# Convolution plus gated projection on one core: the pair loop rotated, the set-up reordered

## The chip, the cores and the metric

The kernel runs on one core of one Trainium2 chip. The metric is the device time of one execution in microseconds (us); three executions of the kernel before took 694.74, 697.43 and 697.51 us, median 697.43.

## What is computed

Input x has 64 sequences, 64 heads and 1024 samples. Two layers follow one another, each added to its input:

```
y = x + (causal convolution of masked x with a 1024-tap kernel per head, built from
         64 complex modes: K = 2 Re sum_n C_n exp(dtA_n t), plus D * x), masked by length
base = y @ W.T                                    # 1024 x 1024
logits = y @ Wr.T + 5 * onehot(language)          # 8 experts
gates = softmax over the two largest logits
out = y + base + 2 * sum_e gates_e * (y @ A_e.T) @ B_e.T   # rank 16 per expert
```

## The kernel before

The heads are handled in 32 **pairs**; a pair is a tile of 128 tokens (two heads of 64 sequences) by 1024 samples in 8 chunks of 128. Every product is made in single precision out of three passes: operands are split into a high part (ACT, a copy rounded to fp32r) and a low part (DVE, the difference), and TensorE (PE) runs hi*hi, hi*lo, lo*hi. The names end in `_hi` and `_lo`.

For one pair PE does this: `turn_rows` (8 transposes of the input rows into `px`), `turn_powers` (2 transposes of the powers Z2 into `ct_psum`, from which come `c_hi`, `c_lo` and the first kernel samples `k_col`), `control` (6 matmuls: the states that enter each chunk, into `px`), `convolve` (6 matmuls with the Toeplitz block `t_hi`, `t_lo`, then 6 with the states `s_hi`, `s_lo`, into `pc`), and the projection: three banks of 24 matmuls with the stationary operand y and the moving operand [W, A, Wr] (1160 columns: bank 2 with the gates' columns first, then bank 0, then bank 1), and three matmuls per bank for the gated low-rank part (`add_lora`), which need the transposed gates.

Between PE's parts stand chains on the other engines. After `control`, ACT copies the states (`copy_states`) and DVE scans them (`scan_states`, eight steps in four pairs, the last three pairs each waiting for ACT to swap halves of the chunk just made, `swap_odd`); then ACT and DVE split them (`split_states`: s_hi, s_lo). After `convolve`, DVE merges the result into xt (`merge`), and ACT and DVE split that (`split_y`). After the first bank, DVE runs `route` (some fifteen small instructions; one waits for ACT's `ratio`), which ends in `gated`. After the banks, ACT copies them to `result` (`finish`, L487 to L488) and issues the output DMAs. Every second step (m = 0 and m = 1 of a loop turn) the powers of the next four heads are made as well: turns, magnitudes and `waves` on ACT at m = 0 (`waves` needs the sine table, L393), `powers`, `swap_powers`, `turn_powers` and `rotate_powers` at m = 1; at m = 1 a one-element Exp (`warm`, L569) brings the exponential table back.

The order of each engine is written by hand; all five engines run freely and wait on semaphores. The loop `Fori(0, LOOPS)` has LOOPS = 14 turns of two steps; step i is pair i's projection, and PE's order in it is: convolve(i+1), bank 2 of i, control(i+2), turn_powers(i+3), bank 0, bank 1 with the gates' transpose, turn_rows(i+3) and the low-rank parts inside it. DVE weaves other work between the four pairs of scan steps (L783): `split_ctr` and `split_obs` of the next pair but one, `split_toe` (t_lo, L749) and `split_gated`.

Ahead of the loop the set-up computes parameters on DVE (`par_step`), turns 11 weight tiles (`TILE`; W in 8 tiles, A, Wr, B) by `turn_weight`, each then split by ACT (`weight`, L370) and DVE (`low_weight`, L737), and convolves pair 0. Projection begins only in the loop, when all tiles are split.

## Time and profile before

| | |
|---|---|
| three executions | 694.74, 697.43, 697.51 us (median 697.43) |
| profiled execution | 695.72 us, of which the span from first to last instruction is 693.9 us |
| PE matmul busy | 645.8 us (93%), 3621 instructions |
| DVE busy | 490.0 us (71%) |
| ACT busy | 467.8 us (67%) |
| mean granted TensorE clock | 0.974 of full |

Time outside the span is 1.8 us. In the rows further down the first number is the start in us from the span's start, the second the duration; "[a <-b]" is the idle time of the engine just before and what ended it. Instructions that follow one another without a wait overlap by about 0.1 us, so that distances between starts, not durations, add up.

### The profile page before, as it was taken

To read this page: it belongs to the slowest core of one execution; us is meant where nothing else is said; L and a number is where in the kernel's file an instruction comes from. 1 tells how busy PE (TensorE), PEld (TensorE's weight loads), DVE (VectorE), ACT (ScalarE), POOL (GpSimd) and SP (SyncE) were. 2 spreads that over 40 slices of the span, in tenths; PEclk is the share of its full clock that TensorE was granted. 3 is DMA by queue.
4 is the path that set the end of the run, shared out by engine and by line. 5 is a ranking of instruction groups with operands and counts; after the bars stand their busy time and mean duration, and the time that the engine had idled before them with its cause. 6 is when DMAs were issued, how large, how long until landed. Compare 5 with 4: busy or idle time off the path is not lost.

```text
span 693.9 us, 12598 instructions
## 1 busy us (share of the span) xinstructions
PE 645.8 (93%) x3621; PEld 615.2 (89%) x3621; DVE 490.0 (71%) x1531; ACT 467.8 (67%) x973; POOL 20.4 (3%) x46
## 2 busy tenths in 40 slices
PE   3364999999999999999999999999999999999997
PEld 2353899999999999999999999999999999999997
DVE  8876567777776767777776767777776767777621
ACT  4784577677768677677768677777768677675411
POOL 2000000000000000000000000000000000000000
PEclk9875899999999999999999999999999999999999
DMA  7123023222123233223123233223123223221112
GB/s 241 49 69 89 11 68 70 54 52 68 32 67 68 68 68 68 53 53 68 31 68 68 68 68 68 53 53 68 31 68 68 68 68 68 53 53 39 31 32 60
DMA packets 22869, 43.36 MB, mean 62 GB/s; under 512 B 8104, under 2 KB 13512, under 8 KB 22856
## 3 DMA queue, kind: packets, MB, share of 16 engines
q1 hardware_dynamic: 17576, 26.42, 17.1%
q10 hardware_dynamic: 5280, 16.78, 9.5%
q14 instruction: 7, 0.06, 0.1%
q8 instruction: 6, 0.10, 0.1%
HBM read 26.35 MB, written 16.84 MB: 62 GB/s over the span
## 4 chain that ended last, share of the span: by engine, by line
DVE 36%; ACT 25%; issue 18%; PE 13%; ACTq 6%; DMA 2%; DVEq 1%; SPq 0%
DVE state L783 17%; PE pmg L1104 9%; ACTq L470 5%; ACT result L488 4%; ACT u_hi L416 4%; ACT turn L379 3%; ACT L393 3%; DVE y_lo L830 3%; ACT swapped L439 2%; ACT Z L405 2%; DVE Z L770 2%; ACT xt L413 2%; DVE c_lo L764 2%; ACT z_swap L398 2%; PE pc L1029 2%
## 5 line engine op out<-in xcount | busy, mean ns | idle before, releaser
L1104 PE MATMUL pmg<-w_hi,y_hi 128*128 128x388 f32 (+1 forms) x768 | 268.7, 350 | 1.7 <-ACT result L488 0.2
L1104 PE MATMUL pmg<-w_hi,y_lo 128*128 128x388 f32 (+1 forms) x768 | 260.1, 339 | 0.0
L1104 PE MATMUL pmg<-w_lo,y_hi 128*128 128x388 f32 (+1 forms) x768 | 259.8, 338 | 0.0
L1104 PEld LDWEIGHTS pmg<-w_hi,y_hi 128*128 128x128 f32 x768 | 144.3, 188 | 7.5 <-ACT result L488 6.5
L1104 PEld LDWEIGHTS pmg<-w_hi,y_lo 128*128 128x128 f32 x768 | 144.6, 188 | 0.2
L1104 PEld LDWEIGHTS pmg<-w_lo,y_hi 128*128 128x128 f32 x768 | 144.2, 188 | 0.0
L439 ACT ACTIVATE swapped<-state 64x128 f32<-64x128 f32 x192 | 59.3, 309 | 67.1 <-DVE state L783 65.7
L783 DVE SCALAR_TENSOR_TENSOR state<-swapped,scan_tab,state 128x192 f32<-128x192 f32 (+1 forms) x240 | 73.8, 349 | 12.1 <-ACT swapped L439 0.2
L812 DVE TENSOR_TENSOR s_lo<-state,s_hi 128x896 fp32r<-128x896 f32 x32 | 35.0, 1093 | 31.5 <-ACT s_hi L461 31.5
L744 DVE TENSOR_TENSOR u_lo<-xt,u_hi 128x1024 fp32r<-128x1024 f32 x32 | 39.2, 1225 | 24.8 <-ACT u_hi L416 24.8
L461 ACT ACTIVATE s_hi<-state 128x896 fp32r<-128x896 f32 x32 | 30.5, 953 | 35.0 <-DVE state L783 35.0
L783 DVE SCALAR_TENSOR_TENSOR state<-state,scan_tab 128x64 f32<-128x64 f32 x180 | 50.6, 323 | 0.0
L770 DVE SCALAR_TENSOR_TENSOR Z<-z_swap,gen_tab,Z 128x128 f32<-128x128 f32 x56 | 16.0, 347 | 38.8 <-ACT Z L405 38.8
L824 DVE COPY_PREDICATED xt<-valid,pc 128x512 f32<-128x512 int32 x64 | 42.9, 724 | 0.0
L488 ACT ACTIVATE result<-pmg 128x388 f32<-128x388 f32 (+1 forms) x96 | 37.0, 458 | 8.1 <-PE pmg L1079 7.9
L466 ACT ACTIVATE y_hi<-xt 128x1024 fp32r<-128x1024 f32 x32 | 33.5, 1048 | 13.2 <-DVE xt L824 13.2
L830 DVE TENSOR_TENSOR y_lo<-xt,y_hi 128x1024 fp32r<-128x1024 f32 x32 | 39.0, 1220 | 4.0 <-ACT y_hi L466 3.9
L379 ACT ACTIVATE turn<-pos,phase,gen_tab 128x128 f32<-128x128 f32 x56 | 23.1, 484 | 22.6 <-issue 22.6
L1022 PE MATMUL px<-ident,rows 128*128 128x128 f32 x256 | 35.8, 286 | 0.0
L398 ACT ACTIVATE z_swap<-Z 64x512 f32<-64x512 f32 x32 | 20.2, 630 | 19.5 <-issue 19.0
L1022 PEld LDWEIGHTS px<-ident,rows 128*128 128x128 f32 x256 | 32.1, 149 | 1.2
L413 ACT ACTIVATE xt<-px 128x1024 f32<-128x1024 f32 x31 | 31.3, 1010 | 0.7 <-PE px L1022 0.7
(195 smaller groups left out, 1068.1 us busy)
## 6 DMA issues: line engine op xcount, KB each, us to landing
rows<-in_x SPq DMA_DIRECT2D x64, 256.0 KB, 5.1
out<-result ACTq DMA_DIRECT2D x62, 256.0 KB, 3.0
toe<-kpad SPq DMA_DIRECT2D x32, 128.0 KB, 4.5
result<-in_L_cond_W SPq DMA_DIRECT2D x5, 512.0 KB, 7.2
rows<-in_L_cond_W SPq DMA_DIRECT2D x2, 512.0 KB, 7.8
result<-in_L_cond_A SPq DMA_DIRECT2D x1, 512.0 KB, 5.8
b_rows<-in_L_cond_B SPq DMA_DIRECT2D x1, 512.0 KB, 7.0
xt<-in_L_cond_W SPq DMA_DIRECT2D x1, 512.0 KB, 8.8
```

The source lines that it names most:

```text
L379: ins = nc.scalar.activation(turn[:, h, :], pos[:, :], ACT.Identity, bias=phase[:, 0:1], scale=gen_scalar(TURNS, g, h, staged))
L413: nc.scalar.activation(xt[s][:, :, :], px[:, :, :], ACT.Copy).then_inc(xt_ready, 1)
L439: ins = nc.scalar.activation(swapped[out_half, :, chunks, :], source[in_half, :, chunks, :], ACT.Copy)
L470: act.dma_start(bass.AP(out.tensor, (2 * i + h) * LEN + c0, [[HEADS * LEN, SEQS], [1, c1 - c0]]), result[s][h * SEQS:(h + 1) * SEQS, c0:c1 ...
L488: nc.scalar.activation(result[s][:, c0:c1], pm[:, n, 0:c1 - c0], ACT.Copy).then_inc(pm_free, 1)
L744: vec.tensor_tensor(u_lo[s][:, :, :], xt[s][:, :, :], u_hi[s][:, :, :].bitcast(F32), ALU.subtract).then_inc(ulo_ready, 1)
L783: ins = vec.scalar_tensor_tensor(out=state[:, h, chunks, :], in0=source[:, h, at, :], scalar=scan_scalar(name, m if staged else i, h, staged),
L812: vec.tensor_tensor(s_lo[:, :, :, :], state[:, :, :, :], s_hi[:, :, :, :].bitcast(F32), ALU.subtract).then_inc(slo_ready, 1)
L824: ins = vec.copy_predicated(xt[s][:, :, h * SEQS:(h + 1) * SEQS], valid[:, :, :], pc[:, h, :, :])
L830: vec.tensor_tensor(y_lo[s][:, :, :], xt[s][:, :, :], y_hi[s][:, :, :].bitcast(F32), ALU.subtract).then_inc(ylo_ready, 1)
L1022: ins = nc.tensor.transpose(px[:, c, :], rows[s][:, c * P:(c + 1) * P], ident[:, :])
L1104: ins = nc.tensor.matmul(pm[:, n, 0:c1 - c0], y[s][:, c, :], w[:, c, c0:c1], start=(c == 0 and y is y_hi and w is w_hi), stop=(c == CH - 1 ...
```

## The change

**The loop is rotated.** PE's step i is now: turn_powers(i+2), bank 2 of i, bank 0 of i, the gates' transpose (`turn_gates`), convolve(i+1), the low-rank parts of those two banks, control(i+2), bank 1 with turn_rows(i+3) in it. On DVE the scan of pair i+2 runs in one piece behind split_y(i+1), and the next step begins with split_ctr and split_obs, then (m = 1) powers, route, split_rows, split_toe, split_gated and merge. On ACT `finish` is taken apart: the third bank of a pair is copied in the next step (`evacuate`), its DMAs are issued in `store`, `waves` stands ahead of the first two banks' copies, and `warm` has moved from m = 1 to m = 0, between the last `swap_odd` and split_states.

**Two steps are peeled** ahead of the loop (which now has 13 turns from b = 1), each in an order of its own.

**The set-up** is rewritten. A second exact exponential on DVE (14 instructions, `decay_exp`) becomes one ACT Exp. The low part of pair 0's rows is taken from `px` itself; the first two heads' powers go ahead of the other two; the first samples of the first two pairs' kernels come as rows (`kernel_row`: two matmuls with the selector `pick`, through the DRAM tensor `kpad_rows`); B is sorted by ACT and no longer by POOL. W has one more staging buffer (`w0_rows`), and the tiles have another order: those of bank 2 first (A, W6, W7, Wr), and pair 0's banks are projected between the later tiles' transposes, chunk ranges of `project`. DVE's order there is: low parts of tiles 4 to 9 around the scan of pair 1, powers(1) behind tile 9, then route(0, 0), tile 10, merge(0, 1); on ACT the copies of pair 0's first two banks stand ahead of split_y(0, 1) and split_rows(0, 2).

The core of the diff (PE's, DVE's and ACT's steps, PE's set-up):

```diff
-        TILE = [(A_, in_pm, 0), (B_, in_pc, 0), (W_, in_pm, 6), (W_, in_pc, 0), (WR_, in_pm2, 0), (W_, in_pm, 7),
-                (W_, in_pc, 1), (W_, in_pm, 2), (W_, in_pc, 3), (W_, in_pm, 4), (W_, in_pc, 5)]
+        TILE = [(A_, in_pm, 0), (W_, in_pc, 6), (W_, in_pm, 7), (WR_, in_pm2, 0), (W_, in_pm, 0), (W_, in_pc, 1),
+                (W_, in_pm, 2), (W_, in_pc, 3), (W_, in_px, 4), (B_, in_pc, 0), (W_, in_px, 5)]
...
+            store_row(0)
+            sp.wait_ge(pad_stored, 64)
+            load_toe_rows(0)
...
+            sp.wait_ge(px_full, 2)
+            load_w(5)
+            sp.wait_ge(wt_full, w_tile(0) + 1)
+            load_w(4)
             sp.wait_ge(wt_full, w_tile(1) + 1)
             load_rows(0, 2)
-            sp.wait_ge(wt_full, w_tile(2) + 1)
-            load_w(4)
+            sp.wait_ge(wt_full, w_tile(5) + 1)
+            load_rows(0, 3)
...
-            def step(b, m, rows_left=True, ahead=True, kernels=True):
+            copy_states(0, 2)
+            for n in range(3):
+                swap_odd(0, 2, n)
+            split_states(0, 2)
+
+            split_ctr(0, 3)
+            split_obs(0, 3)
+            evacuate(0, 0, 2)
+            split_rows(0, 3)
+            ratios(0, 1)
+            split_toe(0, 2)
+            act.wait_ge(gen_staged, 1)
+            turns_of(None, True)
+            magnitudes(None, True)
+            store(0, 0)
+            split_gated(0, 1)
+            waves(2)
+            evacuate(0, 1, 0)
+            evacuate(0, 1, 1)
+            split_y(0, 2)
+            copy_states(0, 3)
+            swap_odd(0, 3, 0)
+            swap_powers(2)
+            swap_odd(0, 3, 1)
+            turn_powers(2, True)
+            swap_odd(0, 3, 2)
+            nc.scalar.activation(warm[:, :], phase[:, 0:1], ACT.Exp)
+            split_states(0, 3)
+
+            def step(b, m, rows_left=True, kernels=True):
+                if rows_left:
+                    split_ctr(b, m + 2)
+                    split_obs(b, m + 2)
+                evacuate(b, m - 1, 2)
+                if rows_left:
+                    split_rows(b, m + 2)
+                ratios(b, m)
+                split_toe(b, m + 1)
                 if kernels and m == 0:
                     act.wait_ge(gen_staged, b + 1)
                     turns_of(None, True)
                 if kernels and m == 1:
                     swap_powers(b + 2)
-                    turn_powers(b + 2, True)
-                split_y(b, m + 1)
+                store(b, m - 1)
+                split_gated(b, m)
                 if kernels and m == 0:
                     magnitudes(None, True)
+                    waves(b + 2)
                 if kernels and m == 1:
-                    nc.scalar.activation(warm[:, :], phase[:, 0:1], ACT.Exp)
-                ratios(b, m)
+                    turn_powers(b + 2, True)
+                for j in range(2):
+                    evacuate(b, m, j)
+                split_y(b, m + 1)
                 if rows_left:
                     copy_states(b, m + 2)
-                if ahead:
-                    split_ctr(b, m + 3)
-                    split_obs(b, m + 3)
-                if rows_left:
-                    swap_odd(b, m + 2, 0)
-                    split_toe(b, m + 2)
-                    swap_odd(b, m + 2, 1)
-                split_gated(b, m)
-                if rows_left:
-                    swap_odd(b, m + 2, 2)
+                    for n in range(3):
+                        swap_odd(b, m + 2, n)
+                    if kernels and m == 0:
+                        nc.scalar.activation(warm[:, :], phase[:, 0:1], ACT.Exp)
                     split_states(b, m + 2)
-                if ahead:
-                    split_rows(b, m + 3)
-                if kernels and m == 0:
-                    waves(b + 2)
-                finish(b, m)
-
-            with act.Fori(0, LOOPS) as b:
+
+            with act.Fori(1, LOOPS) as b:
                 for m in range(2):
                     step(b, m)
             step(LOOPS, 0, kernels=False)
...
+            next(scanning)
+            split_toe(0, 0, toe_rows_back)
...
+            vec.tensor_copy(len_f[:, :], len_i[:, :]).then_inc(masks, 1)
+            vec.tensor_copy(lang_f[:, :], lang_i[:, :]).then_inc(masks, 1)
+            split_states(0, 0)
             dve.wait_ge(masks, 2)
             vec.tensor_tensor(valid[:, :, :], sample_no[:, :].unsqueeze(2).to_broadcast([P, CH, SEQS]),
                               len_f[:, :].unsqueeze(1).to_broadcast([P, CH, SEQS]), ALU.is_lt).then_inc(masks, 1)
...
-            def step(b, m, rows_left=True, ahead=True, kernels=True):
+            dve.wait_ge(scan_staged, 1)
+            for _ in scan_states(0, 2):
+                pass
+            split_states(0, 2)
+
+            split_ctr(0, 3)
+            split_obs(0, 3)
+            route(0, 1)
+            split_rows(0, 3)
+            split_toe(0, 2)
+            angles(2)
+            split_gated(0, 1)
+            merge(0, 2)
+            powers(2)
+            split_y(0, 2)
+            for _ in scan_states(0, 3):
+                pass
+            rotate_powers(2, True)
+            split_states(0, 3)
+
+            def step(b, m, rows_left=True, kernels=True):
+                if rows_left:
+                    split_ctr(b, m + 2)
+                    split_obs(b, m + 2)
                 if kernels and m == 1:
                     powers(b + 2)
-                merge(b, m + 1)
+                route(b, m)
+                if rows_left:
+                    split_rows(b, m + 2)
+                split_toe(b, m + 1)
                 if kernels and m == 0:
                     angles(b + 2)
+                split_gated(b, m)
+                merge(b, m + 1)
                 if kernels and m == 1:
                     rotate_powers(b + 2, True)
                 split_y(b, m + 1)
-                route(b, m)
-                scanning = iter(())
                 if rows_left:
                     dve.wait_ge(scan_staged, b + m // 2 + 1)
-                    scanning = scan_states(b, m + 2)
-                next(scanning, None)
-                if ahead:
-                    split_ctr(b, m + 3)
-                    split_obs(b, m + 3)
-                next(scanning, None)
...
-                next(scanning, None)
-                if rows_left:
+                    for _ in scan_states(b, m + 2):
+                        pass
                     split_states(b, m + 2)
-                if ahead:
-                    split_rows(b, m + 3)
-
-            with dve.Fori(0, LOOPS) as b:
+
+            with dve.Fori(1, LOOPS) as b:
                 for m in range(2):
...
+            def turn_gates(b, m, tables_split):
+
+                pe.wait_ge(gated_ready, 2 * b + m + 1)
+                pe.wait_ge(clo_ready, tables_split)
+                nc.tensor.transpose(pg[:, 0:P], gated[:, :, :].rearrange("p e r -> p (e r)"), ident[:, :]
+                                    ).then_inc(gt_full, 1)
+
+            def add_loras(b, m):
+
+                pe.wait_ge(gthi_ready, 2 * b + m + 1)
+                pe.wait_ge(gtlo_ready, 2 * b + m + 1)
+                add_lora(BANK_ORDER[0])
+                add_lora(BANK_ORDER[1])
+
...
@@ -1117,50 +1249,101 @@
             pe.wait_ge(par_dve, C2_STEPS)
             pe.wait_ge(prm_ready, 1)
             turn_parameters(C2_RE)
+            pe.wait_ge(z2_half, 1)
             pe.wait_ge(prm_ready, 2)
-            turn_powers(0, 0)
+            turn_powers(0, 0, first=True)
+            pe.wait_ge(tables, 2)
+            kernel_row(0)
+            pe.wait_ge(xt_ready, 1)
             control(0, 0)
-            pe.wait_ge(k_ready, 1)
+            pe.wait_ge(clo_ready, 1)
             turn_powers(0, 1)
+            kernel_row(1)
             turn_weight(2)
+            turn_rows(0, 1)
+            pe.wait_ge(k_ready, 2)
             turn_weight(3)
-            turn_rows(0, 1)
+            pe.wait_ge(wlo_ready, 2)
+            convolve(0, 0, first=True)
             turn_weight(4)
-            turn_weight(5)
-            convolve(0, 0, first=True)
             control(0, 1)
             pe.wait_ge(merged, 1)
+            turn_weight(5)
+
+            wait_y(0, 0)
+            pe.wait_ge(wlo_ready, 4)
+            project(0, 0, 0, 0, 3)
             turn_weight(6)
-            pe.wait_ge(k_ready, 2)
-            pe.wait_ge(clo_ready, 2)
+            project(0, 0, 0, 3, 6)
+            turn_weight(7)
+            pe.wait_ge(v_copied, 2)
+            pe.wait_ge(scan, SCAN + 1)
+            turn_weight(8)
+            project(0, 0, 0, 6, 8)
+            pe.wait_ge(wlo_ready, w_tile(3) + 1)
+            project(0, 0, 1, 0, 4)
+            turn_weight(9)
+            project(0, 0, 1, 4, 8)
+            turn_weight(10)
+            pe.wait_ge(wlo_ready, 10)
+            convolve(0, 1)
+            turn_gates(0, 0, 2)
+            pe.wait_ge(wlo_ready, WTILES)
+            project(0, 0, 2, 0, 4)
+            turn_rows(0, 2)
+            project(0, 0, 2, 4, 7)
+            add_loras(0, 0)
+            project(0, 0, 2, 7, 8)
+            add_lora(BANK_ORDER[2])
             turn_powers(0, 2)
-            for k in range(7, WTILES):
-                turn_weight(k)
-            turn_rows(0, 2)
-
...
+            wait_y(0, 1)
+            project(0, 1, 0, 0, 4)
+            turn_rows(0, 3)
+            project(0, 1, 0, 4, 8)
+            project(0, 1, 1)
+            turn_gates(0, 1, 4)
+            convolve(0, 2)
+            add_loras(0, 1)
+            control(0, 3)
+            project(0, 1, 2, 0, 7)
+            turn_rows(0, 4)
+            project(0, 1, 2, 7, 8)
+            add_lora(BANK_ORDER[2])
+
+            def step(b, m, rows_left=True, ahead=True):
+                if rows_left:
+                    turn_powers(b, m + 2)
+                wait_y(b, m)
+                project(b, m, 0)
+                project(b, m, 1)
+                turn_gates(b, m, 2 * b + m + 3 if rows_left else PAIRS)
                 convolve(b, m + 1)
-                pe.wait_ge(yhi_ready, 2 * b + m + 1)
-                pe.wait_ge(ylo_ready, 2 * b + m + 1)
-                project_bank(b, m, 0)
+                add_loras(b, m)
                 if rows_left:
                     control(b, m + 2)
+                project(b, m, 2, 0, 7)
                 if ahead:
-                    turn_powers(b, m + 3)
-                project_bank(b, m, 1)
-                project_bank(b, m, 2, ahead)
-
-            with pe.Fori(0, LOOPS) as b:
+                    turn_rows(b, m + 3)
+                project(b, m, 2, 7, 8)
+                add_lora(BANK_ORDER[2])
+
+            with pe.Fori(1, LOOPS) as b:
                 for m in range(2):
                     step(b, m)
-            step(LOOPS, 0, kernels=False)
-            step(LOOPS, 1, ahead=False, kernels=False)
-            step(LOOPS + 1, 0, rows_left=False, ahead=False, kernels=False)
-            pe.wait_ge(yhi_ready, PAIRS)
-            pe.wait_ge(ylo_ready, PAIRS)
-            for j in range(3):
-                project_bank(LOOPS + 1, 1, j)
```

**Place 1, DVE in the loop, step m = 0 before** (L783 scan, L749 t_lo, L868 gt_lo; "waits" names semaphores):

```order
L783 SCALAR_TENSOR_TENSOR state<-swapped,scan_tab,state 128x64 [waits swap_ready]
L783 SCALAR_TENSOR_TENSOR state<-swapped,scan_tab,state 128x64
L749 TENSOR_TENSOR t_lo<-toe,t_hi 128x256 [waits thi_ready]
L796 REGISTER_ALU
L783 SCALAR_TENSOR_TENSOR state<-state,scan_tab 128x64 [waits scan]
L783 SCALAR_TENSOR_TENSOR state<-state,scan_tab 128x64
```

t_lo stands here inside the scan. The same engine and turn of the change, step m = 1 (where the former row order had the scan's pieces between these), from split_states on:

```order
L914 TENSOR_TENSOR s_lo<-state,s_hi 128x896 [waits shi_ready]
L855 REGISTER_ALU
L857 TENSOR_REDUCE k_col<-pmg 128x2 [waits chi_ready]
L858 TENSOR_TENSOR c_lo<-pmg,c_hi 128x256
L848 SCALAR_TENSOR_TENSOR zo_lo<-Z,sigma,zo_hi 128x256 [waits zhi_ready]
L723 ISA [waits mag_ready,sin_ready]
L725 TENSOR_TENSOR Z<-angle,mag 128x512 [waits z_swapped,zlo_ready]
L940 TENSOR_TENSOR logits<-pmg,bias 128x8 [waits gate_done]
```

k_col, c_lo and zo_lo have moved from the scan to behind s_lo, and route behind them. The same step of the change from route's last instruction on:

```order
L964 TENSOR_TENSOR gated<-pmg,gates 128x128 [waits router]
L837 TENSOR_TENSOR u_lo<-xt,u_hi 128x1024 [waits uhi_ready,xt_ready]
L842 TENSOR_TENSOR t_lo<-toe,t_hi 128x256 [waits thi_ready]
L970 TENSOR_TENSOR gt_lo<-pmg,gt_hi 128x128 [waits gthi_ready]
L918 COPY held<-lang_f 128x1 [waits conv_done,ulo_ready]
L926 COPY_PREDICATED xt<-valid,pc 128x8x64 x2
```

The Toeplitz block's low part has moved from the middle of the scan to a place behind the whole scan, split_states, route and split_rows.

**Place 2, PE in the loop**, the convolution and what stands ahead of it, before and of the change (L1079 is the low-rank part, L1230 the gates' transpose):

```order
L1079 MATMUL pmg<-bt_hi,gt_hi 128x388
L1079 MATMUL pmg<-bt_hi,gt_lo 128x388
L1079 MATMUL pmg<-bt_lo,gt_hi 128x388
L1029 MATMUL pc<-u_hi,t_hi 128x512 [waits tlo_ready,merged,thi_ready,wlo_ready,ulo_ready,uhi_ready]
L1029 MATMUL pc<-u_lo,t_hi 128x512
```

Here the previous pair's last low-rank matmuls are followed by the convolution. PE of the change:

```order
L1229 REGISTER_ALU [waits gated_ready]
L1230 MATMUL pmg<-ident,gated 128x128 [waits clo_ready]
L1165 REGISTER_ALU
L1159 MATMUL pc<-u_hi,t_hi 128x512 [waits tlo_ready,thi_ready,merged,ulo_ready,uhi_ready]
L1159 MATMUL pc<-u_lo,t_hi 128x512
```

The convolution has moved from the step's head to behind the gates' transpose; it still waits for t_lo.

**Place 3, ACT in the loop**, the table load before (step m = 1, ahead of ratio), and of the change (step m = 0, ahead of s_hi):

```order
L466 ACTIVATE y_hi<-xt 128x1024 [waits merged]
L569 ACT_TABLE_LOAD
L569 ACTIVATE warm<-phase 128x1
L474 ISA
L475 ACTIVATE ratio<-top 128x1 [waits router]
```

Here it stands behind y_hi. ACT of the change:

```order
L479 ACTIVATE swapped<-state 64x2x64
L668 ACT_TABLE_LOAD
L668 ACTIVATE warm<-phase 128x1
L498 REGISTER_ALU
L501 ACTIVATE s_hi<-state 128x896 [waits conv_done,scan]
```

The load has moved from beside split_y to between the last swap and the split of the states.

## Rows read from the trace of the kernel before

**Rows 1.** The page's 40 slices of the span, PE's busy tenths and granted clock

```profile
PE   3364999999999999999999999999999999999997
...
PEclk9875899999999999999999999999999999999999
```

**Rows 2.** The timeline of DVE in the set-up: start, duration, engine, line

```profile
47.63 1.22 DVE L830 TENSOR_TENSOR y_lo<-xt,y_hi 128x1024 fp32r<-128x1024 f32 x1 [0.56 <-ACT y_hi L466]
...
73.34 1.22 DVE L737 TENSOR_TENSOR w_lo<-pc,w_hi 128x1024 fp32r<-128x1024 f32 x1 [4.10 <-ACT w_hi L370]
```

**Rows 3.** The timeline of PE in the loop and near the end

```profile
113.33 0.39 PE L1029 MATMUL pc<-u_hi,t_hi 128*128 128x512 f32 x1
...
308.58 0.39 PE L1029 MATMUL pc<-u_hi,t_hi 128*128 128x512 f32 x1
...
311.18 0.34 PE L1104 MATMUL pmg<-w_hi,y_hi 128*128 128x384 f32 x1
...
315.39 0.36 PE L1029 MATMUL px<-u_hi,c_hi 128*128 128x448 f32 x1
...
327.72 0.39 PE L1029 MATMUL pc<-u_hi,t_hi 128*128 128x512 f32 x1
...
347.63 0.39 PE L1029 MATMUL pc<-u_hi,t_hi 128*128 128x512 f32 x1
...
658.03 0.39 PE L1029 MATMUL pc<-u_hi,t_hi 128*128 128x512 f32 x1
```

**Rows 4.** The timeline of DVE near the end, where it waits for others

```profile
649.90 0.74 DVE L783 SCALAR_TENSOR_TENSOR state<-state,scan_tab,px 128x192 f32<-128x192 f32 x2 [0.57 <-ACT swapped L439]
...
652.19 0.48 DVE L783 SCALAR_TENSOR_TENSOR state<-swapped,scan_tab,state 128x64 f32<-128x64 f32 x2 [0.25 <-ACT swapped L439]
...
660.89 0.15 DVE L816 COPY held<-lang_f 128x1 f32<-128x1 f32 x1 [3.10 <-PE pc L1029]
660.96 1.34 DVE L824 COPY_PREDICATED xt<-valid,pc 128x512 f32<-128x512 int32 x2
```

**Rows 5.** The timeline of DVE in the loop

```profile
302.20 0.28 DVE L763 TENSOR_REDUCE k_col<-pmg 128x2 f32<-128x128 f32 x1
...
303.12 0.47 DVE L783 SCALAR_TENSOR_TENSOR state<-state,scan_tab 128x64 f32<-128x64 f32 x2
...
308.29 1.09 DVE L812 TENSOR_TENSOR s_lo<-state,s_hi 128x896 fp32r<-128x896 f32 x1 [1.02 <-ACT s_hi L461]
...
316.74 0.16 DVE L838 TENSOR_TENSOR logits<-pmg,bias 128x8 f32<-128x8 f32 x1
...
319.01 0.74 DVE L783 SCALAR_TENSOR_TENSOR state<-state,scan_tab,px 128x192 f32<-128x192 f32 x2
...
...
330.49 0.69 DVE L635 TENSOR_TENSOR Z<-angle,mag 128x512 f32<-128x512 f32 x1 [0.81 <-ACT angle L393]
```

**Rows 6.** The timeline of ACT in the loop

```profile
307.30 0.95 ACT L461 ACTIVATE s_hi<-state 128x896 fp32r<-128x896 f32 x1 [1.10 <-DVE state L783]
...
309.07 1.01 ACT L416 ACTIVATE u_hi<-px 128x1024 fp32r<-128x1024 f32 x1
...
314.41 1.04 ACT L466 ACTIVATE y_hi<-xt 128x1024 fp32r<-128x1024 f32 x1
...
317.40 0.58 ACT L447 ACTIVATE state<-px 128x512 f32<-128x512 f32 x1
317.99 0.98 ACT L439 ACTIVATE swapped<-px 64x384 f32<-64x384 f32 x2
...
336.21 1.28 ACT L569 ACT_TABLE_LOAD   x1
337.50 0.20 ACT L569 ACTIVATE warm<-phase 128x1 f32<-128x1 f32 x1
```

**Rows 7.** The waits, whole span: total us, times, longest us

```profile
ACT turn L379 <- issue: 22.6, 13, 1.8
...
ACT z_swap L398 <- issue: 19.0, 14, 1.5
```

488 lines of the change are left out of this document (273 added, 215 removed).

## The prediction

> **What bounds the kernel now.** I read the page's slices first. From the sixth of 40 slices on PE is busy to nine tenths or more at the full granted clock; in the first five it is busy to three to six tenths, and there its clock falls to between 5 and 8 tenths [rows 1]. So there are two places: a set-up of some 75 us that PE waits through, and a loop that PE's own work fills. In the set-up pair 0 is ready for projection at 48.85 us (its y_lo starts at 47.63 and takes 1.22), but the last weight tile's low part ends only at 74.56 [rows 2]: 26 us in which the projection could run and does not.
>
> In the loop I take the start of each convolution as the mark. One step lasts 19.14 us (308.58 to 327.72) and the next 19.91 (to 347.63), 39.05 for a turn of two [rows 3]. The first is PE's work alone. The second holds 0.77 of waiting, around the powers and a late copy on ACT. PE's own pace would be 38.28 a turn.
>
> **What the change does to the order.** The convolution now stands behind two banks, one of which takes 4.21 (311.18 to 315.39) [rows 3]. At the same mark 8.4 us less work is left than before. PE does the same matmuls otherwise; the two selector products and the halves of B cost under 1 us, in a set-up where PE waits anyway. The end (last bank, copy, store) is as before.
>
> **The loop.** The question is whether DVE and ACT close their circle within PE's 19.14. The circle begins at a convolution and ends at the next, because that one waits for t_lo, and DVE makes t_lo only behind the whole scan, split_states, route and split_rows. Counted from the convolution's first matmul:
> - The merge's first instruction comes at 2.86 (658.03 to 660.89) and the merge ends at 4.27 [rows 3, 4]. y_hi follows at 4.31; ACT's next instruction can start 0.95 later (1.04 less an overlap of 0.09), the copy of the states is 0.59 and the swaps 0.98 [rows 6], so the scan starts at 6.86. control's result is there by 4.9 (the low-rank parts and six matmuls behind the convolution), so ACT, not PE, sets this.
> - The scan, now in one piece: 2.29 to the first addition that waits for a swap (649.90 to 652.19) [rows 4]. That addition is 0.48; the next pair takes 0.03 + 0.73 + 0.48 in the same way (0.73 is 2.29 less two steps of 0.78), and the last pair, with no swap left to wait for beyond its first half, 0.03 + 0.78 + 0.75. Sum 5.57. s_hi starts at 12.46.
> - From s_hi: s_lo 0.99 later, the next instruction 1.00 after that [rows 5, 6], k_col, c_lo and zo_lo together 0.92 (302.20 to 303.12). Then route: 2.27 from logits to the instruction behind it (316.74 to 319.01) [rows 5]. u_lo, as large as y_lo [rows 2], 1.13 net; t_lo, a quarter of it, about 0.4; 0.1 until PE starts.
> - At m = 1 powers comes ahead of route, 0.60 (0.69 less 0.09) [rows 5]. 12.46 + 0.99 + 1.00 + 0.92 + 0.60 + 2.27 + 1.13 + 0.4 + 0.1 = 19.87.
> - At m = 0 route waits for ratio. On ACT s_hi and xt take 1.77 (307.30 to 309.07), u_hi 0.91 [rows 6], and between them stand three copies of 256, 256 and 388 columns, about 1.1 (an estimate from xt's 0.91 for 1024): ratio can start 3.8 behind s_hi, and route wants it at 3.5. The loop's turn adds 0.38 on ACT: the idle time that nothing explains is 22.6/13 = 1.74 at the turn and 19.0/14 = 1.36 within it [rows 7]. So 0.68 in place of powers' 0.60: 19.95.
> - warm now stands between the last swap and s_hi, once a turn. From that swap's start s_hi would come after 1.64; with the load of 1.28 and the 0.20 [rows 6] it comes after 2.2. That is 0.5.
>
> Sum 40.3 a turn against 39.05, **1.27 more**. Of this PE is idle 2.0, ahead of each convolution. The former 0.77 goes and is worth nothing. Bounds: at best the three estimated pieces and the register instructions hide each other (0.8 less); at worst the scan's additions in the loop carry another 0.1 each and the waves at m = 0 delay y_hi (0.8 more). The 13 turns between the third mark and the 29th: **+16.5** (6 to 27). The two steps behind it have no powers: +0.4.
>
> A rule against this: the Trainium skill (ScalarE: Activation LUTs, What ACT_TABLE_LOAD costs) has a drain of about 1.38 us beside the load's 1.28. Here the load starts at 336.21, and warm at 337.50, 0.01 behind its end; no row shows the drain [rows 6]. With it warm's 0.5 would be some 1.9.
>
> **The set-up.** Here I followed DVE, ACT and PE through the new orders, each instruction with its duration from before.
> - The 14 dropped DVE instructions (about 0.13 apart) and the split powers bring pair 0's first convolution forward. Pair 0's y_lo is done at about 41, 8 us earlier than in [rows 2].
> - Between 36 and 63 DVE has seven low parts of 1.13, the scan and the splits of pair 1, merge, angles, powers(1) and route, some 23 us of work, and powers(1) must wait for ACT's exponentials. The last tile is split at about 63, 11 us earlier than in [rows 2]. Two of pair 0's banks run beside this, hidden.
> - Then bank 1 of pair 0 (4.3), the turned rows and the low-rank parts end at 69. ACT copies two banks before it makes y_hi of pair 1 and then xt and u_hi of pair 2; DVE's u_lo and c_lo follow, and control of pair 2 starts at 74.3 with PE idle since 70. The slices show the clock at 5 tenths after such holes [rows 1], so it takes 2.3 instead of 1.2. Copy, scan and the chain above (1.6 + 5.6 + 7.1) bring pair 2's convolution, the second mark, to 91.0.
> - The next step carries swap_powers, turn_powers and rotate_powers inside the scan, 1.85 more than 19.95: the third mark falls at 112.8, before 113.33 [rows 3]: **-0.5**. The set-up's 8 to 11 us are spent again in these two steps. Bounds -5 and +4: pieces of the set-up hide better, or half clock again in the next convolution.
>
> **Sum.** 693.9 - 8.4 - 0.5 + 16.5 + 0.4 = 701.9 of span, with the 1.8 outside it 703.7, against the profiled execution's 695.72. Its time lies inside the three runs shown, 1.7 under their median, so I leave the sum at its level: **704 us**, 1% over the median. A measurement here can tell about 0.5% from no change: faster is under 694, slower over 701.
>
> **Rivals.**
> - *The loop stays PE's* (0.23). If some part of the circle overlaps that I put in a row, the third and later marks keep 39.05: 704 - 16.5 = 687.5, and at PE's own 38.28 677.5. The circle must be 1.0 shorter a step than I count, out of 20. For it: DVE is busy for 71% only. Against it: the waits in the chain are of the kind that rows 4 to 6 show, each with its idle time. It gives faster for 0.20 and same for 0.03.
> - *The clock falls in the loop* (0.06). Each step now has a hole of about 1 us at full clock; the trace of before has none there, and shows falls only in the set-up [rows 1]. A convolution of 2.60 (308.58 to 311.18) [rows 3] takes as much again at half clock (1.2 GHz), in 26 steps 68: 772.
> - *A dearer table switch* (0.04). If ACT empties for about another load's length, 1.28, before the load that now has idle neighbours, 13 x 1.28 = 16.6 is added: 720. The rule of the Trainium skill's ScalarE: Activation LUTs (What ACT_TABLE_LOAD costs) would bring it.
> - *The set-up does not do what it says* (0.05). If the rewritten order stalls (staging buffers are freed late, or the strided copy of B), pair 0's banks wait for tiles as they did and only the loop's loss remains: 704 + 8 = 712 or more.
> - *My forecast* (0.62), with its own range of 694 to 716: 0.50 over 701, 0.12 under.
>
> **Numbers.** Faster 0.20; same 0.12 + 0.03 = 0.15; slower 0.50 + 0.06 + 0.04 + 0.05 = 0.65. The range leaves out the clock's case, the top of the dear cases and the lower half of the first rival: 686 to 717.
>
> **What would show it.** PE's timeline of the change: idle times of 0.7 to 1.5 ahead of each convolution's first matmul, released by DVE's t_lo; two marks 40.3 apart over a turn (under 39.0 I am wrong about the circle); s_hi a further 0.5 behind the last addition at m = 0 with the table load ahead of it; DVE with idle times only where it waits for ACT inside the scan. In the set-up: y_lo of pair 0 ending near 41, the last low part near 63, a hole in PE near 70 to 74, pair 3's convolution near 113. PE idle nowhere ahead of the convolution, or the granted clock under full in the loop, would each prove a rival.

## The result and the profile after

The changed kernel takes 714.6 us (median of 4 executions, 714.37 to 714.98), the kernel before 696.36 in the same session (4 executions): a ratio of 1.0264, 95% interval 1.0238 to 1.0291. It is slower, as forecast, but by 2.6% and not by 1%. Its profiled execution took 714.37 us, the span is 712.6 against 693.9.

| | forecast | measured | miss |
|---|---|---|---|
| third mark against before (112.8 forecast, 120.23 measured, 113.33 before) | -0.5 | +6.9 | +7.4 |
| 13 loop turns between the third and the 29th mark | +16.5 | +19.4 | +2.9 |
| from there to the end | -8.0 | -7.6 | +0.4 |
| span | 701.9 | 712.6 | +10.7 |

The marks are again the first matmuls of the convolutions; the 29th is at 647.18, and was at 620.87 in the kernel before. The timeline of PE of the changed kernel (start, duration; idle time before and its releaser in brackets), rows that answer to [rows 3]:

```profile
91.80 0.76 PE L1159 MATMUL pc<-u_hi,t_hi 128*128 128x512 f32 x1 [1.34 <-DVE t_lo L842]
...
120.23 0.47 PE L1159 MATMUL pc<-u_hi,t_hi 128*128 128x512 f32 x1
...
303.07 0.47 PE L1159 MATMUL pc<-u_hi,t_hi 128*128 128x512 f32 x1 [1.27 <-DVE t_lo L842]
...
322.91 0.47 PE L1159 MATMUL pc<-u_hi,t_hi 128*128 128x512 f32 x1 [0.47 <-DVE t_lo L842]
...
343.61 0.47 PE L1159 MATMUL pc<-u_hi,t_hi 128*128 128x512 f32 x1 [1.27 <-DVE t_lo L842]
...
647.18 0.47 PE L1159 MATMUL pc<-u_hi,t_hi 128*128 128x512 f32 x1 [0.48 <-DVE t_lo L842]
```

Steps of 19.84 and 20.70 alternate; the turn is 40.54 long ((647.18 - 120.23) / 13 = 40.53), where it was (620.87 - 113.33) / 13 = 39.04. In the loop every convolution waits for t_lo, released by DVE. The page's list of waits says the same for the whole span, and shows the one long wait for powers that the forecast had not:

```profile
PE pc L1159 <- DVE t_lo L842: 28.9, 29, 4.3
PE pmg L1201 <- DVE Z L864: 4.2, 1, 4.2
PE px L1159 <- DVE c_lo L858: 4.0, 1, 4.0
```

The slices, against [rows 1]: PE is fuller early (the banks of pair 0 run there), but the fifth and sixth slices fall to 7, and the granted clock is low in two separate stretches of the set-up. In the loop it is full, holes and all.

```profile
PE   3679778999999999999999999999999999999997
...
PEclk9699988999999999999999999999999999999999
```

**The circle in the loop.** The timeline of DVE between the marks 322.91 and 343.61, the step that ends at m = 1:

```profile
325.86 0.15 DVE L918 COPY held<-lang_f 128x1 f32<-128x1 f32 x1 [1.93 <-PE pc L1159]
...
329.96 0.74 DVE L885 SCALAR_TENSOR_TENSOR state<-state,scan_tab,px 128x192 f32<-128x192 f32 x2 [0.33 <-ACT swapped L479]
...
336.90 1.09 DVE L914 TENSOR_TENSOR s_lo<-state,s_hi 128x896 fp32r<-128x896 f32 x1 [1.40 <-ACT s_hi L501]
337.91 0.28 DVE L857 TENSOR_REDUCE k_col<-pmg 128x2 f32<-128x128 f32 x1
...
338.95 0.69 DVE L725 TENSOR_TENSOR Z<-angle,mag 128x512 f32<-128x512 f32 x1
339.56 0.16 DVE L940 TENSOR_TENSOR logits<-pmg,bias 128x8 f32<-128x8 f32 x1
...
341.80 1.22 DVE L837 TENSOR_TENSOR u_lo<-xt,u_hi 128x1024 fp32r<-128x1024 f32 x1
342.93 0.42 DVE L842 TENSOR_TENSOR t_lo<-toe,t_hi 128x256 fp32r<-128x256 f32 x1
```

And ACT's part of the same step:

```profile
327.31 1.06 ACT L506 ACTIVATE y_hi<-xt 128x1024 fp32r<-128x1024 f32 x1
...
333.87 0.63 ACT L479 ACTIVATE swapped<-state 64x128 f32<-64x128 f32 x2 [0.55 <-DVE state L885]
334.52 1.28 ACT L668 ACT_TABLE_LOAD   x1
335.82 0.20 ACT L668 ACTIVATE warm<-phase 128x1 f32<-128x1 f32 x1
335.93 0.94 ACT L501 ACTIVATE s_hi<-state 128x896 fp32r<-128x896 f32 x1
```

Link by link, measured (forecast): convolution to merge 2.95 (2.86), to y_hi 1.45 (1.45), to the scan 2.65 (2.55), scan to s_hi 5.97 (5.60 and 0.5 for the warming Exp), to s_lo 0.97 (0.99), to k_col 1.01 (1.00), to powers 1.04 (0.92), powers 0.61 (0.60), route 2.24 (2.27), u_lo 1.13 (1.13), t_lo and PE's start 0.68 (0.5). Sum 20.70 against 20.37.

**The set-up.** Pair 0's y_lo starts at 39.47 and the last low part at 63.30, 1.2 long each, so that they end at 40.7 and 64.5 (forecast 41 and 63); the second mark is 91.80 (91.0). From there to the third mark it takes 28.43 where 21.8 was forecast. PE's timeline there, then the stretches' busy time (PE first) and granted clock (the 0.50 and 0.78 behind POOL's entry), for the convolution and for the banks in front of the third mark:

```profile
75.61 0.44 PE L1159 MATMUL px<-u_hi,c_hi 128*128 128x448 f32 x1 [4.03 <-DVE c_lo L858]
...
109.09 0.69 PE L1201 MATMUL pmg<-ident,Z 128*128 128x128 f32 x2 [4.20 <-DVE Z L864]
```

```profile
91.80:96.73 4.93, 4.93 (x12) 4.09 (x13) 0.97 (x3) 1.88 (x2) 0.00 (x0) 0.50 0.56 135
109.78:120.20 10.42, 10.42 (x50) 10.38 (x48) 5.58 (x21) 5.16 (x11) 0.00 (x0) 0.78 0.41 84
```

At half the clock, its 1.2 GHz level, the 12 matmuls take 4.93 and not 2.60. And the turn of the powers, with which PE's peeled step (1, 0) begins, stands 4.20 idle with two banks queued behind it, because DVE's rotate_powers(2) comes behind the whole scan of pair 3:

```profile
105.80 0.75 DVE L885 SCALAR_TENSOR_TENSOR state<-state,scan_tab 128x192 f32<-128x192 f32 x2
107.24 0.75 DVE L885 SCALAR_TENSOR_TENSOR state<-swapped,scan_tab,state 128x192 f32<-128x192 f32 x2 [0.69 <-ACT swapped L479]
107.90 1.14 DVE L864 SCALAR_TENSOR_TENSOR Z<-z_swap,gen_tab,Z 128x128 f32<-128x128 f32 x4
```

### The profile page after: what moved, and what is told of

Its sections match the earlier page's. It is cut to its first block, busy times and chain, and to the rows that moved or that the text cites. A ratio compares the mean times of both kernels' runs of the same rounds, so it can differ in the third digit from the quotient of the medians.

```text
span 712.6 us, 12371 instructions
## 1 busy us (share of the span) xinstructions
PE 648.1 (91%) x3629; PEld 617.4 (87%) x3629; DVE 495.3 (70%) x1518; ACT 464.9 (65%) x980; POOL 19.1 (3%) x38
## 4 chain that ended last, share of the span: by engine, by line
DVE 34%; PE 22%; issue 21%; ACT 21%; DVEq 1%; ACTq 1%; DMA 0%; SPq 0%
PE pc L1159 13%; DVE state L885 11%; ACT swapped L479 9%; PE pmg L1220 7%; DVE xt L926 5%; ACT s_hi L501 3%; DVE u_lo L837 3%; ACT state L487 3%; ACT L668 2%; DVE t_lo L842 2%; DVE zo_lo L848 2%; DVE gate L959 1%; DVE held L918 1%; DVE k_col L857 1%; DVE c_lo L858 1%
## 5 line engine op out<-in xcount | busy, mean ns | idle before, releaser
L1220 PEld LDWEIGHTS pmg<-w_hi,y_hi 128*128 128x128 f32 x768 | 145.9, 190 | 4.1 <-DVE w_lo L828 3.6
L524 ACT ACTIVATE result<-pmg 128x388 f32<-128x388 f32 (+1 forms) x96 | 43.2, 452 | 71.8 <-PE pmg L1207 71.3
L918 DVE COPY held<-lang_f 128x1 f32<-128x1 f32 x96 | 14.8, 154 | 78.5 <-PE pc L1159 76.3
L1159 PE MATMUL pc<-u_hi,t_hi 128*128 128x512 f32 x64 | 28.7, 448 | 28.9 <-DVE t_lo L842 28.9
L1159 PEld LDWEIGHTS pc<-u_hi,t_hi 128*128 128x128 f32 x64 | 12.4, 194 | 36.7 <-issue 35.2
L1152 PE MATMUL px<-ident,rows 128*128 128x128 f32 x256 | 34.1, 277 | 1.1 <-DVE state L885 1.1
L1152 PEld LDWEIGHTS px<-ident,rows 128*128 128x128 f32 x256 | 30.5, 144 | 2.4 <-issue 1.2
L456 ACT ACTIVATE u_hi<-px 128x1024 fp32r<-128x1024 f32 x31 | 32.0, 1033 | 0.0
```

Source lines behind the costliest of these rows:

```text
L524: nc.scalar.activation(result[s][:, c0:c1], pm[:, n, 0:c1 - c0], ACT.Copy).then_inc(pm_free, 1)
L1152: ins = nc.tensor.transpose(px[:, c, :], rows[s][:, c * P:(c + 1) * P], ident[:, :])
L1159: ins = nc.tensor.matmul(out, l, r, start=first and n == 0, stop=last and n == 2, skip_group_check=True)
L1220: ins = nc.tensor.matmul(pm[:, n, 0:o1 - o0], y[s][:, c, :], w[:, c, o0:o1], start=(c == 0 and y is y_hi and w is w_hi), stop=(c == CH - 1 ...
```

## The experiments

All are edits of the changed kernel; ratios are to the kernel before in the same session. Times of different sessions are compared below where the text says "less" or "slower", and the kernel before had medians of 696.27 to 697.58 in them: a difference of 1 us between two such times says nothing by itself.

**1. toe_first: t_lo ahead of u_lo.** The circle's theory says that the loop's loss hangs on what stands ahead of t_lo. DVE's step:

```diff
                 route(b, m)
+                split_toe(b, m + 1)
                 if rows_left:
                     split_rows(b, m + 2)
-                split_toe(b, m + 1)
```

> One swap on DVE: in every loop step t_lo is made ahead of u_lo of the next pair but one, so 1.13 us earlier. Theory (the next convolution waits for t_lo at the end of DVE's and ACT's circle): the step into m = 0 loses its wait of 0.48 and the step into m = 1 loses 1.13 of its 1.27; a turn falls from 40.53 to about 38.95 us, the span by 13 x 1.58 + 0.5 + 0.5 = 21.5, the time to about 693. Rival (PE's new order itself, or its matmuls being longer, costs the turn): the turn stays near 40.5 and the time near 714.

Measured 690.95 us, ratio 0.9901 (0.9876 to 0.9926): one line moved turns 2.6% of loss into 1% of gain. A turn lasts 38.70, a little less than the 38.95 expected.

**2. toe_early: t_hi and t_lo right behind the splits of zo, ahead of powers, route and the rows' split.** On ACT t_hi goes behind zo_hi, on DVE

```diff
+                split_toe(b, m + 1)
                 if kernels and m == 1:
                     powers(b + 2)
                 route(b, m)
                 if rows_left:
                     split_rows(b, m + 2)
-                split_toe(b, m + 1)
```

> t_hi (ACT) and t_lo (DVE) are made right behind the next pair but one's zo, ahead of powers, route and the rows' split, some 4 us earlier than in the change. Theory: the wait ahead of each convolution is gone in both steps and the turn is PE's own, about 38.8 us (19.43 + 19.36 from the change's trace); time about 691. If another link of the circle (the gates' transpose, the states' low part) is late next, the turn stays above 39 and PE's wait moves to that instruction. Rival (PE's order costs): 714.

Measured 690.06, ratio 0.9904 (0.9886 to 0.9922), no better than the first. PE's timeline shows no idle time ahead of the convolutions.

```profile
312.89 0.48 PE L1159 MATMUL pc<-u_hi,t_hi 128*128 128x512 f32 x1
...
332.46 0.47 PE L1159 MATMUL pc<-u_hi,t_hi 128*128 128x512 f32 x1
```

Steps of 19.57 and 19.13 alternate, a turn of 38.70 against 40.54: 13 x 1.84 = 23.9 of the 24.5 us. The two former waits, 1.27 and 0.47, are gone in both experiments. The step of 19.57 is still 0.45 longer than the other, and not by PE's own work: here the gates' transpose ahead of its convolution starts 0.40 behind the last matmul of the bank (331.82 to 332.22; in the other step 0.19), and the convolution 0.24 behind the transpose (0.02). In toe_first the transpose is on time (334.31), and the convolution starts 0.46 behind it. In either order DVE's route and t_lo both stand ahead of this convolution, which fits the equal turns. Experiment 10 takes this step up again.

**3. late_turn: the turn of the powers behind the first bank, in the peeled step only.**

```diff
-                if rows_left:
+                if rows_left and not late:
                     turn_powers(b, m + 2)
                 wait_y(b, m)
                 project(b, m, 0)
+                if late:
+                    turn_powers(b, m + 2)
                 project(b, m, 1)
...
-            with pe.Fori(1, LOOPS) as b:
+            step(1, 0, late=True)
+            step(1, 1)
+            with pe.Fori(2, LOOPS) as b:
```

> Only PE's order in the loop's first step changes: the transposes of pair 4's powers stand behind that step's first bank instead of at its head. Theory for the third mark (pair 3's convolution at 120.23 us in the change's trace, 7.4 later than predicted): PE waited 4.2 us at its head for rotate_powers(2), which DVE makes behind the whole scan, with two banks queued behind the wait; now the first bank runs in that wait, the convolution comes at about 115.5, bound by DVE's chain again, and the time falls by 4.8 to about 709.7. Rival (the late third mark is the half clock and the slow convolution at 91.8 alone): third mark at 119 to 120, time 714.

Measured 709.81, ratio 1.0192 (1.0171 to 1.0212): 4.8 less. The wait for the powers is gone (107.49, no idle time), the third mark comes 23.18 behind the second, not 28.43, and the convolution waits for t_lo as in the loop:

```profile
107.49 0.44 PE L1201 MATMUL pmg<-ident,Z 128*128 128x128 f32 x2
...
114.36 0.47 PE L1159 MATMUL pc<-u_hi,t_hi 128*128 128x512 f32 x1 [1.34 <-DVE t_lo L842]
```

With the late turn the circle of DVE and ACT binds this step again. Its 23.18 is 1.4 more than the 21.8 forecast, and the convolution at its head took 3.86 (91.18 to 95.04, granted clock 0.66) where 2.60 is its length at full clock: that is 1.3 of it.

**4. no_warm: the warming Exp left out.** The line with `warm` in ACT's loop is deleted; the load then falls to ratio at m = 1.

> The one-element Exp between the last swap and the states' high part at m = 0 is left out; the table load then stands ahead of ratio at m = 1 (the result is the same). Theory: s_hi at m = 0 comes 0.5 us earlier, but ratio at m = 1 about 1.0 later than route wants it, so the step into m = 1 is about 0.5 longer than 20.70 and the time about 720. If a table switch costs a further drain of the order of 1.4 us beside its 1.28, the step is longer by that again (some 738). If s_hi was not bound by warm, the step grows by 1.0 (727).

Measured 723.77 in a single run, 9.2 slower. The step that ends at m = 1 lasts 21.28 instead of 20.70, 7.5 in 13 turns; the third mark comes 0.9 earlier (119.29). Another 2.9 come from two of the other steps, which last 21.40 (from 140.57) and 21.13 (from 347.69) and not 19.84: the granted clock was 0.92 over each, and 0.55 from 140.57 to 143.00. Both times PE had just waited 0.43 and 1.27; the other turns of this kernel have the same two waits, and their steps keep 21.28 and 19.84. The load now stands on the path to route:

```profile
301.77 1.28 ACT L510 ACT_TABLE_LOAD   x1
303.06 0.30 ACT L510 ACTIVATE ratio<-top 128x1 f32<-128x1 f32 x1
```

Where it stood, load and Exp cost 0.40 (the scan's start to s_hi is 5.97 with them and 5.57 in the other step of the same trace, 350.64 to 356.21). Here the step is 0.58 longer although these 0.40 are saved, so 0.98 show. The next instruction starts 0.01 behind the load's end, here as in the changed kernel: the dear switch is out.

**5. early_late: 2 and 3 together.**

> Two edits at once: t_hi and t_lo early in the steps of the loop (alone 690.06), and PE's turn of the powers behind the first bank in its peeled first step (alone 4.8 under the changed kernel, 709.81 against 714.6). The first takes 1.84 from each turn of the loop, the second only from the stretch between the convolutions of pair 2 and pair 3, so they should add: 690.06 - 4.8 = 685.3, with loop turns of 38.70. If instead the 4.8 was only won because the loop's DVE behind it was late anyway (the loop of that kernel waits for t_lo), or if PE's order there only moves the wait, 690.0.

Measured 685.89, ratio 0.9844 (0.9827 to 0.9861). The two losses, loop and peeled step, add: 4.2 of the second's 4.8 are left on top of the first.

**6. act_order: in ACT's set-up, pair 1's y_hi ahead of the copies of pair 0's banks.**

```diff
-            evacuate(0, 0, 0)
-            evacuate(0, 0, 1)
             split_y(0, 1)
             split_rows(0, 2)
+            evacuate(0, 0, 0)
+            evacuate(0, 0, 1)
```

> The changed kernel with one thing altered in ACT's set-up: y_hi of pair 1 and the copy and u_hi of pair 2 stand ahead of the two bank copies of pair 0 instead of behind them. ACT waits 3.18 idle for the first bank's last LoRA there, while the merged rows of pair 1 have been ready since about 65.2; y_hi could start near 65.9 and not 69.8, c_lo of pair 2 end near 71 and not 74.6, and PE's hole of 4.03 ahead of control(0,2) close to under 1. Theory (ACT's order makes the hole): control(0,2) starts at about 71.5, the second mark moves from 91.8 to about 88, and the whole kernel gains 3.5 to 5 (the stretch at half clock behind the hole may go too): 710.5. Rival (the next limit, the copies of the banks moved behind, holds project(0,1,0) back as long, or the time is lost at the next wait for gates): 713.5 or more.

Measured 711.67, ratio 1.0211 (1.0191 to 1.0231): 2.9 less, between theory and rival. The hole of 4.03 is down to 1.22 and the second mark comes at 89.17 (from 91.80), but a part came back at the next wait: the gates of pair 1, for which PE now waits 2.88 and not 1.92.

**7. fill: PE's two waits ahead of the convolution of pair 2 filled.** It adds work that computes nothing:

```diff
             project(0, 1, 1)
+            pe.wait_ge(clo_ready, 4)
+            for n in range(34):
+                nc.tensor.transpose(ct_psum[:, n % 2, :], ident[:, :], ident[:, :])
             turn_gates(0, 1, 4)
             convolve(0, 2)
```

> The changed kernel with 34 transposes of the identity added to PE's two waits ahead of the convolution of pair 2 (idle 1.92 and 1.34 there; 34 x 0.10 = 3.4). They compute nothing. Theory: that convolution took 4.93 and not 2.6 because the granted clock was 0.50 behind the two waits; with the waits filled it starts at 91.9 and takes about 2.7, the merge of pair 2 comes 2.2 earlier, and the kernel ends 2 earlier: 712.4. Rival 1: the clock falls all the same (it was 0.66 and 0.72 in two other kernels with the same waits), and nothing changes: 714.6. Rival 2: the filler only delays the gates' turn and what follows by its overshoot: 715.5.

Measured 711.72, ratio 1.0215 (1.0198 to 1.0232): PE does more and the kernel ends 2.9 earlier. The convolution's stretch at full clock (1.00), 2.66 long where it was 4.93, and the banks ahead of the third mark at 0.86:

```profile
91.34:94.00 2.66, 2.65 (x12) 2.32 (x13) 0.98 (x3) 2.05 (x3) 0.00 (x0) 1.00 0.67 90
107.00:116.50 9.50, 9.50 (x49) 9.50 (x48) 5.57 (x21) 5.17 (x11) 0.00 (x0) 0.86 0.32 61
```

The wait for the powers stays, 4.43. So the 6.6 us have two causes that are now each shown alone, this and experiment 3. How far the clock falls is not steady, but that it falls is: in eight kernels with both waits left (1.92 to 2.88 and 1.20 to 1.37) the 12 matmuls of this convolution took 4.93 or 4.94 at 0.50 (the changed kernel, toe_first, early_late, act_order, warm_gap) or 3.86 to 3.88 at 0.66 (toe_early, late_turn, no_warm); in none of them did the convolution as a whole run at full clock.

**8. full: 2, 3 and 6, and t of pair 2 ahead of its route in the set-up.**

> All orders together: t early in the loop (-24.5), PE's late turn of the powers in its peeled step (-4.8), ACT's y_hi and u_hi ahead of the bank copies in the set-up (-4), and t_hi and t_lo of pair 2 ahead of the route in the set-up (-1.3, the wait ahead of the convolution of pair 2): 714.6 - 34.6 = 680.0. If the set-up's orders overlap (what ACT's order wins is lost at the gates of pair 1, whose route stands behind the scan of pair 2): 684.

Measured 680.39, ratio 0.9763 (0.9748 to 0.9778), as the sum said. Between the control of pair 2 and the third mark one long wait of PE's is left, for the gates of pair 1:

```profile
87.90 0.47 PE L1230 MATMUL pmg<-ident,gated 128*128 128x128 f32 x1 [3.21 <-DVE gated L964]
88.11 0.77 PE L1159 MATMUL pc<-u_hi,t_hi 128*128 128x512 f32 x1
...
104.49 0.44 PE L1201 MATMUL pmg<-ident,Z 128*128 128x128 f32 x2 [0.24 <-DVE Z L864]
```

**9. warm_gap: the warming Exp behind the copy of the states,** where ACT idles for 1.67 (alone, in the changed kernel):

```diff
                     copy_states(b, m + 2)
+                    if kernels and m == 0:
+                        nc.scalar.activation(warm[:, :], phase[:, 0:1], ACT.Exp)
                     for n in range(3):
                         swap_odd(b, m + 2, n)
-                    if kernels and m == 0:
-                        nc.scalar.activation(warm[:, :], phase[:, 0:1], ACT.Exp)
```

> The changed kernel with the warming Exp of the loop put behind the copy of the states instead of between the last swap and s_hi. ACT is idle there for 1.67 in each turn (the first swap of the scan waits for DVE), and load and Exp take 1.39. Theory (the circle over DVE and ACT sets the step, link by link): s_hi follows the last addition 0.40 earlier, the m = 1 step shortens from 20.70 to 20.30, the other stays at 19.84; 13 x 0.40 = 5.2 less: 709.4. Rival (what the warm delays is covered by some other wait behind it, the ratio or the copies): 714.6. If the load in the gap also delays the first swap (a drain beside the 1.28), the gain is under 2: 712.6 or more.

Measured 711.01, ratio 1.019 (1.0164 to 1.0215), 3.6 less and not 5.2. The loop did what the theory said: the step is 20.31 to 20.33 instead of 20.70, the other stays at 19.84. The load fits in the gap:

```profile
328.53 0.98 ACT L479 ACTIVATE swapped<-px 64x384 f32<-64x384 f32 x2
329.53 1.28 ACT L666 ACT_TABLE_LOAD   x1
330.83 0.20 ACT L666 ACTIVATE warm<-phase 128x1 f32<-128x1 f32 x1
331.18 0.63 ACT L479 ACTIVATE swapped<-state 64x128 f32<-64x128 f32 x2 [0.15 <-DVE state L885]
```

The profiled execution has its second mark at 93.43 and its third at 121.78, each 1.6 later than the changed kernel with the same set-up, and that is what is missing of the 5.2. The granted clock accounts for it. The 43 matmuls behind the last tile's low part took 8.61 at 0.80 (63.63 to 72.24) and not 7.01 at 1.00 (64.57 to 71.58); the control of pair 2 and what follows it to the gates' transpose took 1.0 more (76.27 to 91.76 against 75.61 to 90.13); ahead of both warm_gap was 0.9 earlier. Why the clock fell in this stretch in one kernel and not in the other stays open.

**10. full_warm: 8 and 9 together.**

> All orders together (680.39) and the warming Exp in the gap. One step of a turn still lasts 19.57 to 19.58 there and not 19.12: its gates come 0.25 late, at m = 1, where the warming Exp and the powers both stand ahead of the route. Theory: with 0.40 of it gone, both steps last 19.12 to 19.2, 13 x 0.4 = 5 less: 675.4. Rival (the 0.45 is PE's own, the branch at the turn of the loop): 680.4.

Measured 675.23, ratio 0.9678 (0.9654 to 0.9702). Steps of 19.12 and some 19.20 now alternate: the longer step was no branch of PE's. In full its gates' transpose stood 0.24 late (323.74, the last matmul of the bank at 323.32 and 0.18 to the next); here it is on time (322.02 behind 321.85), and the 0.40 of the Exp was what made it late.

**11. full_warm_route: the route of pair 1 directly behind the scan of pair 2,** in DVE's set-up (on ACT its ratio goes behind split_states likewise):

```diff
             for _ in scan_states(0, 2):
                 pass
-            split_states(0, 2)
-
+            route(0, 1)
             split_ctr(0, 3)
-            split_obs(0, 3)
             split_toe(0, 2)
-            route(0, 1)
+            split_states(0, 2)
+            split_obs(0, 3)
             split_rows(0, 3)
```

> The previous kernel and, in the set-up, the route of pair 1 directly behind the scan of pair 2, with its ratio behind s_hi; c_lo, t_lo, s_lo behind the route. PE waits 3.21 for these gates; they need only the route (2.3) and c_lo (0.6) behind the scan's end and come about 2.7 earlier. Theory: the wait falls to about 0.5, the convolution of pair 2 starts at 85.5 and its clock holds: 2.5 to 3.5 less, 672.5. Rival (the states' low part, 2.9 later than before, holds the convolution's second half or the control of pair 3): 675.

Measured 673.66, ratio 0.9657 (0.9634 to 0.968), 1.6 less. The wait fell from 3.20 to 0.62, the second mark from 88.52 to 86.22, and the convolution behind the shorter wait ran at full clock. A wait of 1.06 for gt_lo is new, ahead of the low-rank parts. The profiled executions differ by 2.3 (third marks 110.85 and 108.53), the medians by 1.6, because full_warm's profiled execution is the slowest of its four:

```profile
85.78 0.30 PE L1229 MATMUL pmg<-ident,gated 128*128 128x128 f32 x1 [0.62 <-DVE c_lo L858]
86.22 0.47 PE L1158 MATMUL pc<-u_hi,t_hi 128*128 128x512 f32 x1
...
300.74 0.48 PE L1158 MATMUL pc<-u_hi,t_hi 128*128 128x512 f32 x1
...
319.93 0.47 PE L1158 MATMUL pc<-u_hi,t_hi 128*128 128x512 f32 x1
```

The turn is 38.3 long, PE's own pace of [rows 3], and all work of the changed kernel is done: same matmuls, only in another order on three engines. It is 3.4% faster than the kernel before and, by the two ratios (0.9657 / 1.0264), 5.9% faster than the change as given. In the page's slices PE has nine tenths from the seventh on and the full clock from the fourth:

```profile
PE   3697989999999999999999999999999999999997
...
PEclk9689999999999999999999999999999999999999
```

## Why the prediction was right and wrong

- **The direction and the mechanism in the loop were right.** "DVE makes t_lo only behind the whole scan, split_states, route and split_rows": the idle times ahead of each convolution are 1.27 and 0.47, released by t_lo, and both went when t_lo moved (experiments 1 and 2). Only one of them lies in the 0.7 to 1.5 named as the sign. The rival in which the loop stays PE's is refuted. The clock's fall in the loop did not happen in the changed kernel (slices at full clock), but no_warm shows that it can: behind the same hole of 1.27 the clock fell in 2 of 26 steps, at 1.3 and 1.6 us each and not the 2.6 in every step of the rival.
- **The loop's term was 2.9 short of 19.4.** The m = 0 step was 19.95 and is 19.84. The m = 1 step was 19.87 and 0.5, and is 20.70. The short terms are in links taken from rows of another neighbourhood: the convolution to the merge (0.09), y_hi to the scan (0.10), the small splits (0.12) and "0.4; 0.1 until PE starts", which is 0.68. The warming Exp was 0.1 too dear (0.40, measured twice: 5.97 less the 5.57 of the other step, and experiment 9). The upper bound of 0.8 a turn held them.
- **The step of the sum that failed is "the third mark falls at 112.8".** It went wrong in the last item of the set-up, "the next step carries swap_powers, turn_powers and rotate_powers inside the scan, 1.85 more than 19.95". Their price on DVE's and ACT's circle was counted. Who else waits for them was not: PE's turn of those powers heads the next step, with two banks behind it in PE's queue, so the wait of 4.20 falls on PE and not beside it. The circle of DVE and ACT, on which I had set the mark, was not binding there: the convolution at 120.23 follows the banks without idle time. The mark moved by +6.9 against the kernel before, which is outside the term's bounds of -5 and +4. The second half is the clock. "Half clock again in the next convolution" was in the bounds and not in the sum, and happened: 4.93 for 2.60, and a clock of 0.78 in the banks behind the wait. Filling the two waits ahead of it took 3.2 off this stretch (28.43 to 25.22), the late turn 5.25. The two overlap and their shares cannot be added exactly, because the clock differs between kernels.
- **The rest of the set-up was right**: y_lo of pair 0, the last tile within 1.5, the hole of 4 us ahead of control of pair 2, the second mark within 0.8. The last is in part luck: kernels with the same set-up have it between 90.90 and 93.43. The rival in which the set-up fails, 712 or more, comes near the measured time by its number only: pair 0's banks did run between the tiles, and what was lost was lost between the second and the third mark. One detail differs: control of pair 2 started at full clock (its first matmul is 0.44 long), and the half clock came a little later.
- **The table switch** cost what its row said. The rule of the Trainium skill (ScalarE: Activation LUTs, What ACT_TABLE_LOAD costs) of a drain of some 1.38 beside the load is not borne out: the instruction behind the load starts 0.01 to 0.02 after the load's end, at 303.06 and 335.82, and the load starts 0.02 after the swap ahead of it ends (333.87 + 0.63 = 334.50). Had the drain been there, the load would not have fitted in the gap of experiment 9.
- **What I missed altogether** is how small the change's flaw was. I argued that PE's 8.4 us were won once and 1.27 lost in each turn, and stopped there. PE stood idle for 1.27 and 0.47 a turn only, and 1.13 of DVE's work on the circle, u_lo of the pair after the next, was needed by nothing that PE waited for at that place.

## What to carry to other kernels

When work is moved behind a long chain, list for every instruction in the chain's order who waits for it, and put those that PE waits for first: t_lo, 0.42 long, cost 24 us here for standing behind one u_lo. A peeled step needs the same list as the loop, since operations that are apart in the loop (powers at m = 1) meet there. And a wait of some us on PE in a set-up should be priced twice: for itself, and for the work behind it at a lower clock (here 4.93 for a convolution of 2.60).

## What was not expected of the hardware

- Adding 34 transposes that compute nothing made the kernel 2.9 us faster, because the granted clock behind them was 1.00 and not 0.50 (the kernel ran 711.05 to 711.86 in four executions, the changed one 714.37 to 714.98).
- Holes of 1.27 at each turn of the loop left the clock full over 26 steps of the changed kernel, but in no_warm it fell behind two of them; in the set-up two waits of 1.92 and 1.34 with a single transpose between them were followed by half clock.
- How far the clock fell behind the same two waits differed between kernels: 0.50 in the changed kernel (waits of 1.92 and 1.34; 91.80 to 96.73), 0.66 in late_turn (2.28 and 1.37; 91.18 to 95.04), the shorter first wait with the lower clock. Marks so shift by 1 to 2 us between kernels with the same set-up, as in warm_gap.
